# Two fused cross-attentions on one core: first and last bodies reordered, the row term spread through DRAM, projections by column block

## What is computed

```python
q = x @ Wq0 + bq0                    # 512 x 512
k = ctx @ Wk0 + bk0;  v = ctx @ Wv0 + bv0
w = softmax(q @ k.T / sqrt(512), over the tokens t)      # first layer: axis 1
x = layernorm(w @ v + x) * gamma + beta
Q = x @ Wq1 + bq1
K = ctx @ Wk1 + bk1;  V = ctx @ Wv1 + bv1
a = softmax(Q @ K.T / sqrt(512), over the context rows)  # second layer
out = x + (a @ V) @ Wo1 + bo1
```

## Time and profile before

| | before |
|---|---|
| median of 3 runs | 698.74 us (698.52 to 698.81) |
| profiled execution, its own time | 701.1 us |
| its span, first to last instruction | 699.0 us |
| TensorE busy | 678.4 us, 97% |
| VectorE, GpSimd, ScalarE busy | 516.6, 488.6, 430.3 us |
| mean granted TensorE clock | 0.993 |

### The profile page before, as it was taken

The page is one execution under the profiler, slowest core; times in us unless marked ns, Lnnn a source line. Parts: engine busy times, 40 slices in busy tenths (PEclk is TensorE's granted clock), DMA queues, the critical chain, the costliest instruction groups (busy, mean ns, idle before and its releaser), DMA issues.

```text
span 699.0 us, 12504 instructions
## 1 busy us (share of the span) xinstructions
PE 678.4 (97%) x4107; PEld 598.0 (86%) x4107; DVE 516.6 (74%) x1235; ACT 430.3 (62%) x1040; POOL 488.6 (70%) x391
## 2 busy tenths in 40 slices
PE   8977999999999999999999999999999999999967
PEld 7864898889889898989889888988889888988856
DVE  4999587677958677786868777795868768686845
ACT  2654557667566757666575766666674766657432
POOL 0267777859586876949587786959687795955680
PEclk9999899999999999999999999999999999999999
DMA  8800104031030404022040403013040402101003
GB/s 298 304 1 18 73 2 151 1 113 38 23 127 0 150 0 150 0 67 83 0 150 0 150 0 129 21 46 104 0 150 0 150 0 96 54 1 60 1 1 121
DMA packets 30336, 49.50 MB, mean 71 GB/s; under 512 B 2160, under 2 KB 10352, under 8 KB 30320
## 3 DMA queue, kind: packets, MB, share of 16 engines
q1 hardware_dynamic: 30320, 49.29, 20.4%
HBM read 32.51 MB, written 16.78 MB: 71 GB/s over the span
## 4 chain that ended last, share of the span: by engine, by line
PE 88%; DVE 6%; POOL 2%; issue 1%; ACT 1%; DMA 1%; SPq 0%; DVEq 0%; POOLq 0%
PE bank L392 75%; PE bank L399 12%; DVE n L839 1%; PE bank L412 1%; DMA wk_sb<-in_L_xattn_Wk_dram 1%; DVE rb L928 1%; POOL x_even L1194 1%; POOL wq_sb L1158 1%; DVE n L1006 1%; POOL wq_sb L1154 1%; DVE stats L995 0%; DVE xT_lo L815 0%; POOL rstd L1164 0%; DVE x_even L990 0%; POOL prod L1171 0%
## 5 line engine op out<-in xcount | busy, mean ns | idle before, releaser
L1171 POOL TENSOR_TENSOR prod<-n,u_b 128x512 f32<-128x512 f32 x64 | 81.4, 1295 | 39.8 <-DVE n L1006 39.8
L813 DVE SCALAR_TENSOR_TENSOR y_lo<-bank,terms,y_hi 128x512 fp32r<-128x512 f32 x64 | 45.8, 751 | 76.6 <-ACT y_hi L637 76.6
L637 ACT ACTIVATE y_hi<-bank,terms 128x512 fp32r<-128x512 f32 x64 | 43.9, 689 | 55.0 <-PE bank L392 55.0
L1210 POOL TENSOR_TENSOR r<-r,beta_b 128x512 f32<-128x512 f32 x60 | 75.9, 1293 | 0.0
L1203 POOL TENSOR_TENSOR r<-n,gamma_b 128x512 f32<-128x512 f32 x60 | 75.6, 1300 | 0.0
L1164 POOL TENSOR_TENSOR rstd<-var_eps,minus_half 128x2 f32<-128x2 f32 x32 | 22.3, 698 | 74.3 <-DVE var_eps L1002 74.2
L639 ACT ACTIVATE pc_hi<-bank 128x512 fp32r<-128x512 f32 x32 | 19.1, 598 | 68.2 <-PE bank L392 68.2
L392 PE MATMUL bank<-xT_hi,wqk_hi 128*128 128x512 f32 x128 | 52.4, 410 | 2.0 <-DVE xT_lo L815 2.0
L392 PE MATMUL bank<-nT_hi,wqk_hi 128*128 128x512 f32 x128 | 50.7, 396 | 3.0 <-DVE nT_lo L815 3.0
L392 PE MATMUL bank<-wv_hi,wc_hi 128*128 128x512 f32 x128 | 51.6, 403 | 1.7 <-issue 1.7
L979 DVE SCALAR_TENSOR_TENSOR r<-bank,rinv,r 128x512 f32<-128x512 f32 x60 | 44.8, 748 | 11.3 <-PE bank L392 11.3
(11 more groups left out here) (197 smaller groups left out, 2363.7 us busy)
## 6 DMA issues: line engine op xcount, KB each, us to landing
out_dram<-r SPq DMA_DIRECT2D x15, 1024.0 KB, 5.0
x_even<-in_x_dram SPq DMA_DIRECT2D x8, 1024.0 KB, 7.1
ctxn<-in_ctx_dram SPq DMA_DIRECT2D x16, 512.0 KB, 3.6
x_odd<-in_x_dram SPq DMA_DIRECT2D x8, 1024.0 KB, 6.6
wq_sb<-in_L_xattn_Wq_dram SPq DMA_DIRECT2D x4, 256.0 KB, 3.4
wk_sb<-in_L_xattn_Wk_dram SPq DMA_DIRECT2D x2, 512.0 KB, 7.0
wv_sb<-in_L_xattn_Wv_dram SPq DMA_DIRECT2D x2, 512.0 KB, 9.0
wq_sb<-in_L_xattn_Wq_dram SPq DMA_DIRECT2D x1, 1024.0 KB, 11.2
```

The costliest lines, as they stand in the source:

```text
L637: i = act.activation(dst, at((name, k))[:], ACT.Identity, bias=bias)
L813: i = dve.scalar_tensor_tensor(dst, src, bias, high.bitcast(F32), ALU.add, ALU.subtract)
L1171: pool.tensor_tensor(prod[j % 2][:], N[:, j, :], u_b[1][:], ALU.mult).then_inc(prod_ready, 1)
L1210: pool.tensor_tensor(r[:, j, :], r[:, j, :], beta_b[:], ALU.add).then_inc(resid_ready, 1)
```

## The change

In words:

- Row term: only the first pair's is spread by TensorE (`spread_first_r0`). For all others SyncE writes `r0s` to a DRAM tensor of 512 values (16 bytes from each partition), waits for that, waits until GpSimd has used `RB` as a bias, and reads it back to all partitions. The values stand in DRAM as (p, j), so `maxima0` reads `RB` with a step of four values.
- `project` does all four k of one column block and ends it before it begins the other; `scores0` waits for the second block of y only before its first use.
- First body: beta·Wq1 goes from VectorE's dots to GpSimd (`beta_products`) and ScalarE (`beta_terms`); GpSimd begins `cut_ctx` only when r0s is there; the product of `bv_wo` goes to ScalarE, its two sums (`bv_wo_sums`) to the end of GpSimd's body; `bo1` comes after both `wvo` tiles; VectorE does the low parts of `wqk1` and the first of `wc` earlier, Wk1·bq1 (`column_terms1`) and `finish_beta` at its end; x of the second pair is loaded ahead of Wo1.
- Last bodies: the output tile 1 of pair 14 also becomes a late one, behind the transposes of n; GpSimd's four row products of pair 15 come after all four rows are normalised, and ScalarE's row terms after it has rounded nT.

```diff
-STEADY = (tiles("xT", 4) + tiles("cT", 2) + tiles("y", 2) + tiles("nT", 4) + tiles("rb", 1) + tiles("s0", 2)
+STEADY = (tiles("xT", 4) + tiles("cT", 2) + tiles("y", 2) + tiles("nT", 4) + tiles("s0", 2)
-LATE = (2, 3)
+LATE = (1, 2, 3)
...
+            def write_r0(ready, spread_before):
+                sp.wait_ge(r0s_ready, ready)
+                if spread_before is not None:
+                    sp.wait_ge(rb_loaded, spread_before)
+                sp.dma_start(r0_rows.rearrange("(p j) -> p j", p=P), r0s[:]).then_inc(r0_written, 16)
+            def spread_r0(written, biased):
+                sp.wait_ge(r0_written, written)
+                sp.wait_ge(x_biased, biased)
+                sp.dma_start(RB[:], r0_rows.partition_broadcast(P)).then_inc(rb_loaded, 16)
...
                     sp.dma_start(ctxn[:], rows_of(ctx_rows, upcoming)).then_inc(ctx_loaded, 16)
+                    write_r0(r0_made, r0_spread)
+                    spread_r0(r0_in_rows, rb_free)
                 if it.back and not it.before_last and not it.last:
...
-                dst = [begin(it, name, c) for c in range(KC)]
-                for k in range(KD):
-                    wait_emptied(pe, it, source, k)
-                    for c in range(KC):
+                for c in range(KC):
+                    dst = begin(it, name, c)
+                    for k in range(KD):
+                        if c == 0:
+                            wait_emptied(pe, it, source, k)
                         w = [h[:, k, c * P:(c + 1) * P] for h in wqk]
...
+                if it.last:
+                    apply(it, "late", 1, "pc", PC, WVO)
+                if begin_it:
+                    spread_first_r0(it)
...
+                row_term = RB[:].rearrange("q (j p) -> q j p" if begin_it else "q (p j) -> q j p", j=J)
...
-                        i = dve.tensor_tensor_reduce(E0[:, b, mt, :], at(("s0", b))[:, mt * T:(mt + 1) * T],
-                                                     RB[:, b * T:(b + 1) * T], -1.0, -LOWEST, ALU.add, ALU.min,
+                        i = dve.tensor_tensor_reduce(E0[:, b, mt, :].rearrange("q (j p) -> q j p", p=P),
+                                                     probs0(b, mt).rearrange("q (j p) -> q j p", p=P),
+                                                     row_term[:, b * RT:(b + 1) * RT, :], -1.0, -LOWEST, ALU.add, ALU.min,
...
+            def beta_products():
+                pool.wait_ge(rows_in_or_stored, 16 * ROWS)
+                pool.wait_ge(dots_ready, KD + KC + 1)
+                for e in range(KD):
+                    wait_emptied(pool, Iteration(PAIRS, 0), "wqT1", e)
+                    pool.tensor_tensor(N[:, e, :], wqT1[:, e, :], beta_b[:], ALU.mult).then_inc(betaq_products, 1)
...
-                    row_products(it, (2, 3), 1)
+                    row_products(it, range(J) if it.last else (2, 3), 1)
```

More of the change, by code:

```diff
@@ L467, in prepare1c @@
                                          for h in range(KD)]), "wvo", c)
[L468 to L471, removed]
+                pe.wait_ge(bvwo_ready, KD + 2)
+                dst = begin(it, "bo1")
+                end(product(dst[:], [(ones_r[:].bitcast(F32), bvwo[:, 0, :])]), "bo1")
             def transpose_inputs(it):
@@ L515, in scores0 @@
                         part = dst[:, mt * T:(mt + 1) * T]
-                        terms = []
                         for c in range(KC):
-                            terms += passes([h[:, c, m0:m0 + P] for h in ct],
-                                            [h[:, c, b * T:(b + 1) * T] for h in Y])
-                        mm = product(part, terms)
+                            if (b, mt, c) == (0, 0, 1):
+                                wait_emptied(pe, it, "y", 1)
+                            mm = product(part, passes([h[:, c, m0:m0 + P] for h in ct],
+                                                      [h[:, c, b * T:(b + 1) * T] for h in Y]),
+                                         first=c == 0, last=c == KC - 1)
                     end(mm, "s0", b)
@@ L756, in iteration @@
                         cut_v0(it)
-                if it.back:
+                if it.back and not it.last:
                     row_terms(it, (2, 3), 1)
@@ L796, in iteration @@
                     next_row_terms0(it)
-                if it.front:
+                if it.front and it.back and not it.before_last:
                     row_terms(it, (0, 1), 0)
@@ L915, in finish_beta, with low_wvo @@
                    .then_inc(emptied[BANK["bo1", 0]], 1)
-            def prepare1c(it):
-                for c in range(KC):
-                    low_weights(it, "wvo", c, [[h[:, c, :] for h in WVO]], [at(("wvo", c))[:]], [1.0])
+            def low_wvo(it, c):
+                low_weights(it, "wvo", c, [[h[:, c, :] for h in WVO]], [at(("wvo", c))[:]], [1.0])
             def first_row_terms0():
@@ L1058, in norm_and_output @@
                         dve.wait_ge(stats_ready, it.times(J, J))
-                    output(it, 1)
+                    if not it.before_last:
+                        output(it, 1)
                 if it.front and not it.before_last:
@@ L1063, in norm_and_output @@
                     aggregate(1)
-                    if not it.back:
-                        finish_beta(it)
                 if it.back and not it.before_last:
@@ L1095, in iteration @@
                         low(it, "nT", k, NT[1][:, k, :], NT[0][:, k, :], per=KD, back=1)
+                if it.last:
+                    output(it, 1, "late", before_last)
                 if it.front:
                     maxima0(it)
-                if begin_it:
-                    beta_wq1(it)
-                if it.front:
                     normalise0(it)
@@ L1103, in iteration @@
                     row_terms1(it)
+                    prepare1b(it)
+                    add_betaq(it)
+                    low(it, "wc", 0, halves(WC[1], 0), halves(WC[0], 0), per=2)
                 if it.back:
@@ L1224, in iteration @@
                     add_beta(it, range(J))
-                if it.j is None and it.known == 0:
-                    bv_wo()
                 if it.front:
```

166 lines of the change are left out of this document (99 added, 67 removed).

## The result

| | before | after |
|---|---|---|
| median, same chip, four runs each | 698.63 us (697.84 to 698.81) | 683.14 us (682.45 to 683.61) |
| profiled execution, own time | 701.1 us | 682.88 us |
| its span | 699.0 us | 680.8 us |
| mean granted TensorE clock | 0.993 | 0.997 |

The ratio is 0.9772, 95% interval 0.9755 to 0.9789: 15.5 us faster, where 14.7 was forecast. A second measurement of the same kernel on another chip gave 0.9801 (0.9779 to 0.9823), 14.4 us. The sum came out right, in part by luck: as the experiments show, in the middle a gain put too high for one edit met one put at nothing for another, and at the ends the first pair gave more than forecast and the last pair less.

The account below looks back on a forecast made before the run. TensorE was taken as the bound, busy 678.4 of 699.0 us. Row term 6.6, first pair 1.3 and its clock 1.4, last pair 5.4 sum to 14.7, so 698.74 - 14.7 = 684.0 us; range 681.5 to 690.0.

Parts of the forecast that it names:

- Row term (-6.6): Pairs 2 to 16: TensorE loses four transposes of 0.44 us in each of 15 pairs, 6.6 us less.
- Projections by column block (0 in the middle): Middle pairs: same 24 matmuls; the first y can be rounded earlier but nothing waited for it, so 0.
- Strided read (0): VectorE's maxima reading RB in 16-byte steps: added time e near nothing, at most 0.35 us each; cost 0.
- the limit of 0.31: Time added to each of four maxima, in us, at which the row sums' wait for w_lo would appear.
- a margin of 1.0: Middle pair: time in us from the end of GpSimd's w_lo sum (287.58) to the row sums' start (288.59).
- GpSimd's idle 0.68: Time in us that GpSimd idles ahead of the w_lo sum, counted as slack against a late store.
- SyncE's queue (0): Row term's DRAM write and read, about 4 to 5 us, are hidden; the store behind is delayed up to 1 us; cost 0.
- The rival's mechanism: SyncE's queue holds the store, delaying GpSimd down to w_lo; 7.5 us lost at 2.2 us delay; chance 0.04.
- First pair (-1.3 and -1.4): First body: projection of pair 2 starts at 67.9 instead of 69.19, 1.3 us; half of 2.9 us clock loss regained, 1.4.
- Last pair (-5.4): Last body: earlier transposes and projection, clock staying up, so scores at 675.0 against 680.42, 5.4 us less.
- if it does fall, 1.7 comes back: Last body: if the clock falls after TensorE's remaining 2.0 us wait, 1.7 us of the gain is lost.

Follow-up runs that it names:

- e5: The kernel before with the row term of pairs 2 to 16 through DRAM and the projections by column block with the late wait: 692.20 us, 0.9892 of before.
- e6: The kernel before with the row term through DRAM and only the scores' late wait for the second block of y: 691.77 us, 0.9894 of before.
- e1: The kernel before with only the row term of pairs 2 to 16 through DRAM: 696.59 us, 0.9951 of before.
- e2: The kernel before with only the projections by column block and the scores' late wait: 700.09 us, 1.0003 of before.
- e8: The kernel after with two more strided maxima on VectorE in each of pairs 2 to 16, result unused: 700.64 us, 1.0014 of before.
- e7: The kernel after with the row term written to DRAM in the scores' order, 512 elements of 4 bytes, so RB is read without a step: 792.70 us, 1.1336 of before.
- e11: The kernel after with output tile 1 of pair 14 back in its own body: 682.07 us, 0.9763 of before.
- e3: The kernel after with the last two bodies as before: 688.22 us, 0.9834 of before.
- e4: The kernel after with the first body as before, except that its row terms still reach the next pair through DRAM: 688.46 us, 0.9837 of before.

## Why the prediction was right, and where it was not

- **Row term (-6.6).** Measured 7.4 and 7.9 us (e5, e6), 7.0 in the traces, but only together with the late wait: "As TensorE is the bound: 15 x 0.44" forgot that the four transposes also covered y_lo. Alone it is 3.3 (e1).
- **Projections by column block (0 in the middle).** The failed step is "nothing waited for it there". True before (e2), false once the row term is gone: 3.3 to 4.1 us, all of it the late wait's (e6). The two errors cancel in the sum, since the edits came together; that is luck.
- **Strided read (0).** "I take e near nothing" was wrong: 0.19 us, within the bounds of 0 and 0.35, hidden. The rule of the Trainium skill cited ahead ("SBUF — State Buffer", "Specifications (TRN2)") pointed the right way. How the limit of 0.31 follows from a margin of 1.0, the prediction doesn't work out; if GpSimd's idle 0.68 is in it, that is time in which GpSimd waits for VectorE, and no cover for it. The rows of after put it at 0.29 by the row sums (0.19 and a quarter of the 0.38 left); e8 is well beyond both, and no run lies near them.
- **SyncE's queue (0).** Write 1.4 and read 3.8 us, "about 4 to 5" for both; the store isn't late at all, 32.6 us after the start of the transposes of n, before 33.1. The rival's mechanism is real: it appears in e7, where the store is 8.1 us late.
- **First pair (-1.3 and -1.4).** The term for the waits was too small: 2.7 in the traces. The shape was right (q1 at 39.3 for 39.1, `pr` at 45.4 for 45.7, the normalisations held by the sum), but GpSimd's sums took 57.41 to 61.2 and not 58.25 to 62.4, so `bo1` started at 61.2 and not 62.4, and beta_b was done at 65.3, not 67.0. The clock gave 1.6; the lower level fell on `bo1` and the transposes, as supposed.
- **Last pair (-5.4).** 5.4 in the first trace of after; 3.7 where the clock falls after the 1.97 us wait. The prediction's proviso, "if it does fall, 1.7 comes back", gave that size (12.07 less 10.41). But the forecast leant on the first pair of before, where the clock had stayed up after a wait of 2.11, and that is a single case: in e1, at the same place, it fell after 2.12 (mean 0.72 in the next 6.2 us, against 1.00 before). That the late tile helps was wrong; with the deferred row products alone (e11) the ratio is 0.9763, with neither (e3) 0.9834. The two orders in the deferral, GpSimd's and ScalarE's, were not taken apart.

So 6.6 + 2.7 + 5.4 = 14.7 was met by 7.4 + 4.0 + 3.7 = 15.1 (e5, e3, e4), against 14.4 and 15.5 measured. That the first pair's surplus of 1.3 and the last pair's lack of 1.7 cancel is luck too.

## What to carry to other kernels

Work on the bounding engine can also be the cover of a wait: before taking it out, look at what the next instruction waits for and when that arrives, and move that wait to its first real use. Moving work behind a wait helps only if the gap behind it is as long as the work; if what is waited for comes at a fixed time, leave the work ahead. Where the bounding engine waits for a reduction on another engine, let it do the reduction if it is shorter than the wait and what it blocks.

## What was new about the hardware

- A VectorE operation over 128x256 with one fp32 input from PSUM and one from SBUF in steps of 16 bytes took 611 ns, without the step 420.
- A DRAM write of 2 KB landed in 1.4 us as 128 pieces of 16 bytes, while as 512 of 4 bytes it held the queue's next instruction for up to 10.3 us.
- After a TensorE wait of 1.94 to 1.97 us ahead of the same transposes the granted clock fell to its lower level in four profiles and stayed up in two; after 0.61 us it stayed up in both.
- Two VectorE normalisations of 128x512 took 3.95 us while GpSimd added two halves of 128x1024, and 1.00 us without that sum.
